# A gated depthwise convolution with GDN on one core: TensorE's keep-awake products, the next image's taps and the order of the last squares are rearranged

## What is computed

```python
pooled = x.mean(axis=(2, 3))
t = relu(gamma * (pooled @ w1.T - running_mean) * rsqrt(running_var + EPS) + beta)   # 24 values per image
wt = (t @ w2.T + b2).reshape(b * DIM, 1, 3, 3) * MASK                                # 4 taps a channel
out = conv(x, wt, depthwise, padding 1) + bias
denom_sq = einsum('nchw,ic->nihw', out * out, gamma_eff) + beta_eff
y = out * rsqrt(denom_sq)
```

## Time and profile before

| | us |
|---|---|
| median of 3 runs | 209.8 |
| lowest and highest | 209.55, 210.91 |
| the profiled execution's own time | 208.62 |
| its span, first to last instruction | 206.7 |
| busy: DVE, PE, ACT, POOL | 187.8, 175.8, 154.6, 150.1 |

### The profile page before, as it was taken

The page is one execution under the profiler, slowest core; times in us unless marked ns, Lnnn a source line. Parts: engine busy times, 40 slices in busy tenths (PEclk is TensorE's granted clock), DMA queues, the critical chain, the costliest instruction groups (busy, mean ns, idle before and its releaser), DMA issues.

```text
span 206.7 us, 2968 instructions
## 1 busy us (share of the span) xinstructions
PE 175.8 (85%) x1037; PEld 66.7 (32%) x1037; DVE 187.8 (91%) x185; ACT 154.6 (75%) x174; POOL 150.1 (73%) x85
## 2 busy tenths in 40 slices
PE   0016894999999999999999999999999999948980
PEld 0014531333354333333543333335433323203320
DVE  3799699959999999999998999999989999999792
ACT  2435453569995979999959899999496959588671
POOL 4000033307899999999999999989999998878600
PEclk9999998599999999999999999999999999997998
DMA  6999959905999999999999999975647657277477
GB/s 200 419 411 405 413 200 331 285 2 145 272 333 298 329 345 359 361 350 370 351 328 340 328 347 385 340 297 140 244 95 290 182 209 262 109 222 289 151 270 237
DMA packets 16581, 58.09 MB, mean 281 GB/s; under 512 B 2388, under 2 KB 2391, under 8 KB 16567
## 3 DMA queue, kind: packets, MB, share of 16 engines
q1 hardware_dynamic: 14256, 51.72, 68.8%
q10 hardware_dynamic: 2310, 6.19, 11.2%
HBM read 26.45 MB, written 25.17 MB: 250 GB/s over the span
## 4 chain that ended last, share of the span: by engine, by line
PE 41%; DVE 30%; POOL 8%; DMA 6%; issue 6%; ACT 4%; SPq 3%; ACTq 1%; DVEq 0%; POOLq 0%
DVE psum L655 18%; PE psum L602 15%; PE psum L585 12%; DVE y L655 11%; DMA ximg<-in_x 6%; POOL work L714 5%; PE psum L616 3%; POOL work L708 3%; SPq L303 3%; PE psum L493 3%; PE psum L552 2%; PE psum L583 2%; ACT work L477 2%; PE psum L488 1%; ACT work L455 1%
## 5 line engine op out<-in xcount | busy, mean ns | idle before, releaser
L714 POOL TENSOR_TENSOR work<-y,work 128x1024 f32<-128x1024 f32 x44 | 103.6, 2375 | 11.2 <-ACT work L477 11.0
L655 DVE SCALAR_TENSOR_TENSOR psum<-ximg,taps,psum 128x1024 f32<-128x1024 f32 x81 | 104.2, 1287 | 5.1 <-PE psum L585 2.3
L602 PE MATMUL psum<-work,gam_e 96*32 96x512 f32 x540 | 83.4, 605 | 5.3 <-ACT work L477 3.5
L603 PE MATMUL psum<-sqd,gam_e 96*32 96x512 f32 x180 | 83.1, 606 | 0.0
L708 POOL TENSOR_TENSOR work<-y 128x1024 f32<-128x1024 f32 x24 | 45.2, 1892 | 33.0 <-DVE y L655 33.0
L655 DVE SCALAR_TENSOR_TENSOR y<-ximg,taps,psum 128x1024 f32<-128x1024 f32 x47 | 60.2, 1281 | 1.6
L477 ACT ACTIVATE work<-psum,beta_e 128x1024 f32<-128x1024 f32 x45 | 49.7, 1104 | 10.6 <-PE psum L603 10.4
L585 PE MATMUL psum<-ximg,diag 128*128 128x512 f32 x120 | 57.3, 599 | 0.0
L602 PEld LDWEIGHTS psum<-work,gam_e 96*32 96x32 f32 x540 | 21.7, 111 | 59.3 <-issue 56.4
L447 ACT ACTIVATE psum<-ximg,par_s,taps 128x1024 f32<-128x1024 f32 x32 | 38.4, 1201 | 1.1 <-ACT work L455 0.6
L376 ACT ACTIVATE pool_out<-ximg 128x2193 bf16<-128x2193 f32 (+2 forms) x16 | 30.0, 1874 | 8.3 <-DMA ximg<-in_x 8.1
(11 more groups left out here) (72 smaller groups left out, 69.1 us busy)
## 6 DMA issues: line engine op xcount, KB each, us to landing
out_y<-work SPq DMA_DIRECT2D x45, 512.0 KB, 4.0
ximg<-in_x SPq DMA_DIRECT2D x36, 516.0 KB, 7.0
ximg<-in_x SPq DMA_DIRECT2D x12, 580.5 KB, 7.7
sqd<-work ACTq DMA_DIRECT2D x45, 128.0 KB, 4.0
out_y<-work SPq DMA_DIRECT2D x2, 384.0 KB, 3.7
out_y<-work SPq DMA_DIRECT2D x4, 192.0 KB, 3.0
par_s<-in_par ACTq DMA_DIRECT2D x1, 281.0 KB, 4.8
sqd<-y SPq DMA_DIRECT2D x2, 128.0 KB, 2.6
```

What stands on the lines that cost most here:

```text
L602: nc.tensor.matmul(den(n)[own, j:j + BANK], gam_e[:, own], held(n)[0:C, j:j + BANK], start=True, stop=True)
L603: ins = nc.tensor.matmul(den(n)[C:P, j:j + BANK], gam_e[:, s * CD:(s + 1) * CD], sqd[:, t % 2, j:j + BANK], start=True, stop=True)
L655: return nc.vector.scalar_tensor_tensor(out=in_rows(dst), in0=tap_in(n, tap), scalar=tap_w(b, s, tap), in1=in_rows(src), op0=ALU.mult, op1 ...
L714: nc.gpsimd.tensor_tensor(held(n), result(n), held(n), ALU.mult).then_inc(scaled, 1)
```

## The change

- **Unit 1.** The wait for three blocks goes, and there are seven keep-awake products instead of six. They stand behind the base of block 2 as before.
- **The next image's taps.** `tap_sums` is called in the chain unit itself, ahead of the second half of the slot-2 base, and writes into slot 0's place (free once the unit's slot-0 block is convolved) instead of place 3. PE's wait for ACT's copy goes. The first image's slots 1 and 2 keep their place under the name `other_taps_in`.
- **The small layer.** Sums that meet the same weights are taken as two columns of one product: four products, two with two columns, instead of six. The result is two columns; ACT's operation adds them by its accumulator output (`accum_out`), with half the bias in each (`bnw[:, 6:7]`, one more DVE operation at the start).
- **The last units.** Eight keep-awake products stand between the last loop unit and block 42's denominators (after block 44 is convolved), in slot 2, and ACT's base of block 47 waits for them. On ACT, the moves of blocks 42 and 43 go ahead of the square of block 44, and the square of block 47's second half goes ahead of the first two rsqrts of the last blocks.

```diff
         def hid_in(t):
-            return sums(at(t, 2))[:, BANK:BANK + 1]
+            return sums(at(t, 2))[:, BANK:BANK + 2]
...
         def taps_in(t):
+            return sums(at(t, 0))[:, 0:SLOTS * TAPS]
+
+        def other_taps_in():
             return psum[:, SLOTS, BANK:BANK + SLOTS * TAPS]
...
         def hidden(act, b, t):
             act.wait_ge(hid_summed, b + 1)
-            nc.scalar.activation(bnw[:, 5:6], hid_in(t), ACT.Identity, bias=bnw[:, 1:2], scale=bnw[:, 0:1]).then_inc(hid_normed, 1)
+            nc.scalar.activation(hid_parts[:, :], hid_in(t), ACT.Identity, bias=bnw[:, 6:7], scale=bnw[:, 0:1],
+                                 accum_out=bnw[:, 5:6]).then_inc(hid_normed, 1)
...
         def hidden_sums(pe, b, t):
...
-            for i, (_, s) in enumerate(PIECES):
-                if i % 2 == 0 and i // 2 in ON_PE:
-                    ins = nc.tensor.matmul(hid_in(t), fold[:, :, :].rearrange("p t g -> p (t g)"), part[:, i:i + 1],
-                                           start=i == 0, stop=False)
-                else:
-                    ins = hidden_sum(hid_in(t), s, part[:, i:i + 1], False, i == LAST_PIECE)
+            folded = [2 * u for u in ON_PE]
+            own = [[i for i, piece in enumerate(PIECES) if piece[1] == s and i not in folded] for s in range(SLOTS)]
+            pairs = [(fold[:, :, :], folded)] + [(w1r[:, s], i) for s, i in enumerate(own)]
+            pairs = sorted((w for w in pairs if w[1]), key=lambda w: -len(w[1]))
+            for k, (weights, i) in enumerate(pairs):
+                step = i[1] - i[0] if len(i) > 1 else 1
+                ins = nc.tensor.matmul(hid_in(t)[:, 0:len(i)], weights.rearrange("p t g -> p (t g)"), part[:, i[0]:i[-1] + 1:step],
+                                       start=k == 0, stop=k == len(pairs) - 1)
             ins.then_inc(hid_summed, 1)
...
         def tap_sums(pe, b, t):
             pe.wait_ge(hid_ready, b + 1)
-            pe.wait_ge(normed, at(t - 2, 2) + 1)
+            pe.wait_ge(convolved, at(t, 0) + 1)
...
             square(act, LAST - 2)
             rsqrt(act, LAST - 6)
-            square(act, LAST - 1)
             move_d(act, LAST - 3)
             move_d(act, LAST - 2)
+            square(act, LAST - 1)
...
             rsqrt(act, LAST - 4)
+            act.wait_ge(kept_awake, 1)
             base_on_act(act, LAST + 2)
...
             square_last(act, 2)
+            square_last(act, 3)
             rsqrt_last(act, 0)
             rsqrt_last(act, 1)
-            square_last(act, 3)
...
                 chain = u == TAPS_UNIT and b < B - 1
-                if u == 0 and b > 0:
-                    tap_sums(pe, b, t - 1)
-                    pe.wait_ge(taps_ready, b + 1)
                 if t == 1:
-                    pe.wait_ge(convolved, SLOTS)
-                    keep_awake(SLOTS, WAKING)
+                    keep_awake(SLOTS, WAKING + 1)
...
                     denominators(pe, at(t - 2, 2))
+                    tap_sums(pe, b + 1, t)
                     base_on_pe(pe, at(t, 2), (1,))
...
+            pe.wait_ge(convolved, LAST)
+            keep_awake(2, WAKING + 2).then_inc(kept_awake, 1)
             denominators(pe, LAST - 3)
...
+            chained(nc.vector.tensor_scalar(bnw[:, 6:7], bnw[:, 1:2], 0.5, None, ALU.mult))
```

More of the change, by code:

```diff
@@ L102, in conv_gdn @@
         begun = sb("begun", [P, 1])
-        bnw = sb("bnw", [P, 6])
+        hid_parts = sb("hid_parts", [P, 2])
+        bnw = sb("bnw", [P, 7])
         own_tap = sb("own_tap", [P, TAPS])
@@ L156, in conv_gdn @@
         hid_begun = sem("hid_begun")
+        kept_awake = sem("kept_awake")
         hid_normed = sem("hid_normed")
@@ L422, in read_other_taps @@
             act.wait_ge(taps_summed, 1)
-            nc.scalar.copy(taps[:, TAPS:SLOTS * TAPS], taps_in(0)[:, TAPS:SLOTS * TAPS]).then_inc(taps_ready, 1)
+            nc.scalar.copy(taps[:, TAPS:SLOTS * TAPS], other_taps_in()[:, TAPS:SLOTS * TAPS]).then_inc(taps_ready, 1)
             act.wait_ge(taps_ready, 1)
@@ L492, in keep_awake @@
             for _ in range(times):
-                nc.tensor.matmul(psum[:, k, 0:BANK], bias_p[:, 0], ones[:, :], start=True, stop=True)
+                ins = nc.tensor.matmul(psum[:, k, 0:BANK], bias_p[:, 0], ones[:, :], start=True, stop=True)
+            return ins
         def first_hidden_sums(pe):
@@ L514, in first_tap_sums @@
             for s in range(1, SLOTS):
-                ins = nc.tensor.matmul(taps_in(0)[:, s * TAPS:(s + 1) * TAPS], w2_s[:, s], hid[:, :], start=True, stop=True)
+                ins = nc.tensor.matmul(other_taps_in()[:, s * TAPS:(s + 1) * TAPS], w2_s[:, s], hid[:, :], start=True, stop=True)
             ins.then_inc(taps_summed, 1)
```

## The result

| | before | changed |
|---|---|---|
| median (20 runs each, same chip), us | 210.26 | 206.62 |
| lowest and highest, us | 208.37, 214.12 | 205.06, 210.64 |
| profiled execution: own time, span, us | 208.62, 206.7 | 206.82, 204.4 |

The ratio is 0.9835 with a 95% interval of 0.9805 to 0.9865: 1.65% faster, against 2.3% forecast (4.8 of 209.8). The median lies in the stated range, nearer to its upper end of 207.3 than to the stated 205.0.

The account below looks back on a forecast made before the run. DVE, PE and POOL were taken to run abreast, POOL's 41.05 us per image the middle's floor. 1.95 + 1.3 + 1.6 - 0.05 = 4.8 us off the 209.8 median gave 205.0, range 203.6 to 207.3.

Parts of the forecast that it names:

- Part 1: Unit 1: DVE's 2.04 us wait for PE's base of block 5 goes; 1.95 us gained, bounds 1.4 and 2.04.
- Part 2: Three image boundaries: DVE's waits for ACT's base, 1.5 us in three, go; 1.3 us gained, bounds -0.5 and 1.53.
- The price: Image boundaries: moved tap products end the slot-2 base's second half 0.22 us later; 0.2 lost in image 2.
- What would show it: Signs in the profile after: clock 1.00 from 28, no wait for ACT's base at boundaries, no pause from block 47 into scales.
- POOL's floor: Two full images: POOL's work alone forbids less than 41.05 us per image, leaving 0.39 and 0.60 us to gain.
- Part 3: Last units: DVE's waits of 1.44 and about 0.3 us before the last scales shrink; 1.6 us gained, bounds 0.3 and 1.9.
- The open question of the burst's length: Tail: eight keep-awake products last 3.6 us at 0.45 spacing or 1.7 at 0.22; with 3.6 part 3 is 0.3 smaller.
- The last store's landing stays.: Kernel's end: the last store's landing was taken as unchanged, with no size given for any change.
- A: Boundaries: moved tap products make DVE wait 0.2 to 0.6 us, or POOL takes the gain; 206.3 us, chance 0.14.
- B: Unit 1 and tail: the clock falls anyway, bursts filling only part of each hole; 206.7 us, chance 0.10.
- C: All three places: no change within 1%, part 1 giving 1.4, boundaries and tail losing; 209.2 us, chance 0.06.
- D: Tail: slower, the gate already low when the burst begins and staying low from 183 to 197; 213.4 us, chance 0.04.

Follow-up runs that it names:

- the second look: The changed kernel itself run once more on the third group's chip, nothing altered: 206.75 us, ratio 0.9824 to the kernel before.
- early store: The changed kernel with SP's store of block 42 ahead of the 64 KB move of block 47's first half: 205.04 us, ratio 0.9755 to the kernel before.
- no bursts: The changed kernel without its keep-awake products in unit 1 and the tail, and without ACT's wait for them: 207.97 us, ratio 0.9875 to the kernel before.
- unit 1 alone: The kernel before with only unit 1 changed (seven keep-awake products at once, no wait for three blocks): 209.75 us, ratio 0.9966.
- last units alone: The kernel before with only the last units changed (eight keep-awake products, the moved square and moves): 208.84 us, ratio 0.9951.
- boundaries alone: The kernel before with only the image boundaries changed (four products, taps moved ahead, no wait for the copy): 209.35 us, ratio 0.9936.
- stores on ACT's queue: The changed kernel with two of the last stores (quarter pieces 3 and 5) issued by ACT instead of SP: 206.60 us, ratio 0.9769 to the kernel before.
- half tail stores: The changed kernel with stores of blocks 42, 43 and 44 cut to 512 of 1024 columns: 204.79 us, ratio 0.9724 to the kernel before.
- earlier loads: The changed kernel with the next image's loads one unit earlier (FETCH_FROM 1 instead of 2): 207.88 us, ratio 0.9815 to the kernel before.
- half the stores: The changed kernel with stores of blocks 6 to 35 cut to 512 of 1024 columns: 203.98 us, ratio 0.9643 to the kernel before.

## Why the prediction was right, and where it was not

**Part 1, unit 1 (1.95).** Its steps are in the trace. The seven products take 1.68 us, spaced some 0.22, and end at 33.6, the pixel sums start at 34.89, block 5's base does not hold DVE at 42.35, and the first denominators come at 42.62, where 42.3 was worked out from the landing. In the profile 2.04 became 0.15. The figure was taken from one execution: three profiles with the old unit 1 show 2.04, 1.99 and 0.49, a mean of 1.5. The part alone gained at most 1.65 by its interval, so 1.95 was too much. And "its cause goes" named the clock as much as the wait; without the burst the clock did fall, and in that one profile DVE still did not wait. The gain is the removed wait's.

**Part 2, the boundaries (1.3).** The three old waits went as worked out. The price, 0.22 at the base of image 2, appears only where a move has already made PE late. The 0.77 at 105.89 follows PE's wait of 0.99 at 94.81, and the 0.18 of the second look one of 0.58; where PE waits there for 0.49 or less (early store, no bursts), DVE has none. The tap products put 0.69 us ahead of that half (103.06 to 103.75) and the four products save 0.44, so by these numbers I estimate that some 0.25 of the 0.77 are theirs and the rest the move's.

What was missed is said in "What would show it": no wait for ACT's base at the boundaries. In the profiled execution others came in their place, 1.56 us for 1.53, since engines that come earlier meet moves and loads that don't. The step that failed is in the weighing of a wait: moves were priced in unit 0 alone, and "POOL's floor" was the only bound put on the middle, where the DMA share of 0.97 stood in the same rows.

Still the size holds over several executions. With the old order (before, unit 1 alone, last units alone) the middle has 1.53, 2.98 and 2.86, a mean of 2.46. With the new order and the traffic of the middle untouched it has 2.07, 0.98, 1.56, 1.40, 0, 0.33 and 0.45 (boundaries alone, no bursts, changed, changed again, stores on ACT's queue, early store, half tail stores), a mean of 0.97. That is 1.5 us by a few executions, and the part alone measured 0.64% (0.16 to 1.13), or 1.35 of 211.22 us. The profile of before that the sum started from was a favourable one.

**Part 3, the last units (1.6).** DVE's side was right to the tenth: both waits are gone, 1.78 us, ACT's base was not delayed, and DVE goes from block 47 into its scale without a pause. The open question of the burst's length came out on the short side: eight products take 1.90 us from 181.58 (3.6 was the other value), and 1.03 us idle are left behind them. The step that failed is "The last store's landing stays." The last stores land 4.85 and 4.5 behind DVE's end in the two looks at the changed kernel, not 3.45 or 3.4. DVE without pauses hands over its stores faster than the DMA engines drain them (3.28 MB from 191 on, share 0.96 to 0.97 from 194 to 200), and SP holds block 42's store until 191.59, though POOL is through with it at 190.0. The two experiments show it from both sides: less volume gives a drain of 3.2, an earlier start one of 3.7.

**Sum.** With means in place of the single profile: 1.5 + 1.5 + 1.8 from DVE's waits, less 1.25 for the drain (4.7 against 3.4), makes 3.55; the medians differ by 3.64, and 1.65% of 210.26 is 3.5. The forecast's 4.8 lacked the drain, and that is about what it was wrong by. The parts measured alone add up to the same within their noise: 0.34 + 0.64 + 0.49 = 1.47%. But the means rest on two to seven executions each, and DVE's wait at the start goes from 0 to 1.17 us in programs that are alike up to there, so the close match is partly luck. The measured median lies nearest to the times of rivals A and B, but their mechanisms are not what happened. The stated range's lower end of 203.6 doesn't follow from its own numbers (204.3 less 1.2 is 203.1); nothing hangs on it.

Part 1 alone was forecast at 0.93% and brought 0.34%. Its profiled execution (210.34, middle 2.98, tail 3.04) was one of its longer ones. Of its 12 runs, seven have a mean granted clock of 0.984 to 0.987 and took 209.0 us in the mean, the other five 0.975 to 0.980 and 210.8. So the longer dip in the tail looks like that of some executions, not of the change; one profile can't show it.

**Rivals.** A, the tap products as the new wait: no, but for the 0.25 estimated above. Its time of 206.3 was near for another reason. B, the clock falls anyway: the slices stay at the upper level to the end of PE's work in every profile with both bursts, but for those with earlier loads. Not every run was profiled, though: two of the 20 runs of the changed kernel have a mean granted clock of 0.983, where the others have 0.988 to 0.996, and took 209.54 and 210.64. Where the clock fell in them is open. The Trainium skill (TensorE: Matmul & The Clock Gate, The HAM clock gate) says that the moment of the gate is not tied to the kernel's start; the length of a dip does differ here with the same idle time of 3.19 us ahead of it (3.4 us at the lower level in the tail before, 6.8 with unit 1 alone). C and D did not occur.

**A better version.** The early store is the changed kernel with one line moved: 205.04 against 206.75 on the same chip, with ratios to before of 0.9755 and 0.9824. Their intervals overlap by 0.004, but each of them holds the noise of the kernel before as well. Run against run, six each, the means are 205.28 and 206.80: 1.5 us apart with a standard error of 0.4, which is clear of noise. The drain of 3.7 in place of 4.5 explains 0.8 of it; that execution also had fewer waits in the middle, which the moved line can't have caused.

## What to carry to other kernels

When a change lets an engine arrive earlier, look at what it then meets: in a stretch with a DMA share near 1, a move's landing takes the place of the wait removed, and the waits' list calls it "issue" or names an engine that had long been done. At the end of a kernel the path is not the last engine's work plus one landing: look at the bytes and the DMA share of the last stores, and look for an idle DMA window just before them and for the store that stands there behind an unrelated wait. Read the waits of more than one execution before a sum is made to the tenth.

## What the runs showed of the hardware

A 128 KB move between partitions took 2.3 us with the DMA engines quiet (issued at 44.6, share 0.00 before it), 4.7 with half the stores, and 5.7 to 7.3 at a share of 0.97. The flow in the two full images was 336 to 350 GB/s before and 338 to 349 after. One and the same program, up to 175 or 195 us, had DVE waits in its middle of 1.53 and 2.86, or of 0 to 1.56, from one execution to the next. A PE idle time of 2.21 us in unit 1 (1.29 to 1.66 in five other profiles with both bursts) left the granted clock at the upper level, and one of 2.74 at the same place was followed by the lower one (1.2 GHz) for some 3.4 us. Both were waits for a transfer, behind the same program on PE.
